# Cross attention of a six-stage decoder block: projections as three rounded products, with the scaling of the probabilities moved from VectorE to ScalarE

## The chip, the core and the metric

One core of a Trainium2 chip runs the whole program in one launch. The metric is the device time of the launch in microseconds, the median of several runs. TensorE multiplies matrices, VectorE and ScalarE work on 128 partitions of rows, POOL (GpSimd) does small vector work and issues stores, SP (SyncE) issues most transfers. Data are float32.

## What is computed

The input x is 4 batches of 512 rows with 512 features; a context has 512 rows of 256 features. Six stages follow each other, each followed by a residual sum and a layer norm: linear attention, a state-space scan, a ternary feed-forward net, attention over the batch axis, cross attention to the context, and a gated feed-forward net whose weights are looked up in a table of 16 values. The change is in the cross attention (16 heads of 128):

```python
q = (hidden_states @ Wq).reshape(B, Sq, H, D)
k = (encoder_hidden_states @ Wk).reshape(B, Skv, H, D)
v = (encoder_hidden_states @ Wv).reshape(B, Skv, H, D)
q = rmsnorm(q, gq)
k = rmsnorm(k, gk)
scores = jnp.einsum('bqhd,bkhd->bhqk', q, k) * scale
attn = jax.nn.softmax(scores, axis=-1)
out = jnp.einsum('bhqk,bkhd->bqhd', attn, v)
out = out.reshape(B, Sq, H * D)
return out @ Wo
```

## The kernel before

The program is written per engine. Each engine runs its instructions in the order written, and they wait for each other by semaphores. The cross attention (in the code the branch `stages >= 4`, semaphore index 3) goes over the 4 batches c and in each over 16 heads hh.

TensorE, for a batch: keys and values of the first group of four heads (`keys(0)`, `values(0)`, four tiles of 128x512 each, two products a tile), four transposed tiles of x, `queries(0)` (four products), `turn_keys(0)`, `query_squares(0)`. Then for each head: `scores(hh)` (four tiles, into banks 4 to 7), `queries(hh + 1)`, `weighted(hh - 1)` (the product of the previous head's probabilities and values), after heads 1, 5 and 9 `values` of the next group, `turn_keys(hh + 1)`, `query_squares(hh + 1)`, `turn_weights(hh)` (16 transposes of the probabilities p4), and after heads 2, 6 and 10 `keys` of the next group. After head 15 the output projection adds, for each head, four products of oT with a tile `woh` of Wo (line 828). Banks 0 to 2 are a ring for everything but the scores; the table TILES4 gives each tile its number in the ring, and `bank4` waits until the tile three before has been copied out (`a_done`).

ScalarE copies the ring's tiles out (`bring`, line 898) in the same order, and computes the four exponentials of a head (line 1098) with the sum of each row. In a head its order is: exponentials, square and copy of the next queries, copy of the previous head's output oT, values if any, next turned keys kr, four tiles pT of turned probabilities, keys if any.

VectorE, in a head: four maxima (line 1509), each with the bias for the exponential (1513), four reciprocals of the sums (1518), each with the scaling of one tile of p4 (1520), after heads 3, 7 and 11 the scaling of the next group's keys (1494, which `turn_keys` waits for), a piece of the last stage's table look-up (`look_up`, lines 1442 to 1456), the mean square of the next queries (1500), and after heads 2, 6 and 10 the key norms (1483, 1485). POOL raises the mean squares to the power -1/2 for queries (1661) and keys (1654).

SP loads the whole of Wq, Wk and Wv before the stage, the context of the batch, the indices of each look-up, and the tiles of Wo, two ahead.

The order of TensorE and of ScalarE in a head, as written (lines 807 on and 1108 on):

```python
# TensorE
scores(hh)
queries(hh + 1)
weighted(hh - 1)
turn_keys(hh + 1); query_squares(hh + 1)
turn_weights(hh)
# ScalarE
exps(hh)
queries(hh + 1)
bring(oT[:, hh - 1, :], got("o", hh - 1))
turned_keys(hh + 1)
for k in range(NT):
    bring(pT[:, k, :], got("pT", hh, k))
```

## Time and profile before

| | |
|---|---|
| three runs | 2971.68, 2980.09, 2981.98 us, median 2980.09 |
| profiled execution | 2983.97 us, span 2982.3 us |
| TensorE, weight loads | 2723.2 us (91%), 1492.2 us (50%) |
| VectorE, ScalarE, POOL | 1976.1 us (66%), 1107.4 us (37%), 637.5 us (21%) |
| DMA | 145.34 MB, 49 GB/s on average |
| chain that ended last | TensorE 62%, VectorE 19%, issue 10%, POOL 5%, ScalarE 2% |

The busy time of an engine is the time in which it had an instruction in work; matmuls overlap, so the pitch of a series is read from the starts of its rows, not from the length of one. A group in the timeline runs into the next by the end of its last instruction: the start of the next row is the true end. In brackets stands the idle time before a row and who ended it. The cross attention takes about 1360 of the 2982 us, from 1229.6 to 2592.

### The profile page before, as it was taken

The page shows a single profiled execution, that of the slowest core. Times are in us where ns is not written, and L with a number is a line of the kernel's source. Part 1 is how long each engine was busy: PE and PEld are TensorE (multiplying, and loading weights), DVE is VectorE, ACT ScalarE, POOL GpSimd, SP SyncE. Part 2 cuts the span into 40 slices and gives each one's busy share as a digit, 9 for nine tenths or more (in the row PEclk, how much of TensorE's full clock was granted, in tenths as well). Part 3 has the DMA queues.
Part 4 walks back from the last instruction along what each step waited for, and adds up shares of the span by engine and source line. Part 5 has one row for each costly group of instructions (what it writes and reads, how often), then busy time and mean ns, then how long its engine had stood idle before and what let it go on. Part 6 is the DMA issues. An engine that isn't in the chain of part 4 may idle for free.

```text
span 2982.3 us, 28735 instructions
## 1 busy us (share of the span) xinstructions
PE 2723.2 (91%) x8882; PEld 1492.2 (50%) x8882; DVE 1976.1 (66%) x3923; ACT 1107.4 (37%) x2015; POOL 637.5 (21%) x569
## 2 busy tenths in 40 slices
...
DMA packets 67406, 145.34 MB, mean 49 GB/s; under 512 B 8115, under 2 KB 24755, under 8 KB 66230
## 3 DMA queue, kind: packets, MB, share of 16 engines
...
q8 instruction: 75, 1.23, 0.2%
q14 instruction: 77, 0.63, 0.1%
...
## 4 chain that ended last, share of the span: by engine, by line
PE 62%; DVE 19%; issue 10%; POOL 5%; ACT 2%; DMA 1%; SPq 1%; DVEq 0%; POOLq 0%; ACTq 0%
PE bank L492 31%; PE bank L828 7%; DVE h L1249 3%; PE bank L783 3%; POOL h L1586 3%; PE bank L842 3%; PE bank L843 3%; PE bank L846 3%; DVE sm L1509 2%; DVE p L1520 1%; DVE val L1448 1%; PE bank L871 1%; PE bank L612 1%; PE bank L768 1%; PE bank L872 1%
## 5 line engine op out<-in xcount | busy, mean ns | idle before, releaser
L1586 POOL TENSOR_TENSOR h<-du,Bb 128x1024 f32<-128x1024 f32 x128 | 306.3, 2396 | 186.9 <-DVE h L1254 173.4
L1249 DVE TENSOR_TENSOR_SCAN h<-bank,h 128x512 f32<-128x512 f32 x256 | 297.8, 1203 | 21.1 <-POOL h L1586 15.1
L953 ACT ACTIVATE bank<-dt,A 128x512 f32<-128x512 f32 x256 | 176.1, 691 | 329.7 <-DVE h L1249 329.6
L1098 ACT ACTIVATE p<-bank,sm,rq 128x512 f32<-128x512 f32 x256 | 199.1, 778 | 209.9 <-DVE sm L1513 209.9
L492 PE MATMUL bank<-pT,v 128*128 128x512 f32 x512 | 237.3, 607 | 2.9 <-ACT pT L898 2.9
L1661 POOL TENSOR_TENSOR rq<-rq,mhalf 128x4 f32<-128x4 f32 x64 | 65.6, 1024 | 791.0 <-DVE rq L1500 791.0
L209 POOL TENSOR_SCALAR rstd<-mv 128x1 f32<-128x1 f32 x96 | 25.3, 264 | 975.4 <-DVE mv L203 975.4
L492 PE MATMUL bank<-xT,wxq 128*128 128x512 f32 x512 | 230.6, 593 | 3.2 <-ACT xT L898 3.2
L828 PE MATMUL bank<-woh,oT 128*128 128x512 f32 x512 | 223.5, 597 | 9.6 <-DMA woh<-in_Wo 7.6
L492 PE MATMUL bank<-kr,q 128*128 128x512 f32 x512 | 230.6, 593 | 0.0
L612 PE MATMUL bank<-h,ident 128*128 128x512 f32 x256 | 151.0, 674 | 83.4 <-DVE h L1254 83.3
L1509 DVE TENSOR_REDUCE sm<-bank 128x1 f32<-128x512 f32 x256 | 175.3, 685 | 33.9 <-PE bank L492 33.7
L1456 DVE COPY_PREDICATED val<-msk,val 128x258 f32<-128x258 int32 x448 | 173.3, 448 | 27.9 <-DVE val L1456 0.2
L1541 DVE TENSOR_TENSOR h<-bank,sg 128x512 f32<-128x512 f32 (+1 forms) x44 | 30.4, 690 | 226.8 <-PE bank L846 226.8
L1254 DVE TENSOR_TENSOR h<-h,Cb 128x1024 f32<-128x1024 f32 x128 | 174.0, 1359 | 6.6
L1448 DVE TENSOR_SCALAR val<-msk,lx,le 128x258 uint32<-128x258 uint32 x512 | 171.6, 410 | 7.9 <-DVE msk L1444 1.4
L828 PEld LDWEIGHTS bank<-woh,oT 128*128 128x128 f32 x512 | 97.2, 191 | 135.2 <-issue 107.5
L492 PEld LDWEIGHTS bank<-pT,v 128*128 128x128 f32 x512 | 99.5, 195 | 129.0 <-issue 124.7
L492 PEld LDWEIGHTS bank<-xT,wxq 128*128 128x128 f32 x512 | 96.9, 190 | 124.7 <-issue 120.5
L195 DVE TENSOR_TENSOR rsum<-bank,xc 128x512 f32<-128x512 f32 x64 | 43.9, 687 | 170.2 <-PE bank L828 165.4
L898 ACT ACTIVATE pT<-bank 128x512 f32<-128x512 f32 x256 | 132.8, 602 | 42.2 <-PE bank L783 42.2
L492 PEld LDWEIGHTS bank<-kr,q 128*128 128x128 f32 x512 | 93.2, 190 | 97.6 <-issue 97.6
...
## 6 DMA issues: line engine op xcount, KB each, us to landing
...
x_dram<-xo POOLq DMA_DIRECT2D x16, 1024.0 KB, 4.7
xc<-x_dram SPq DMA_DIRECT2D x16, 1024.0 KB, 5.2
woh<-in_Wo SPq DMA_DIRECT2D x64, 256.0 KB, 2.7
...
xc<-in_x SPq DMA_DIRECT2D x4, 1024.0 KB, 7.4
```

Of the source, the lines that this page charges most:

```text
L492: m = pe.matmul(dst, l, r, start=(k == 0), stop=(k == len(pairs) - 1))
L612: pe.matmul(bank[4 + et][:, :], ident[:, :], h[:, U % HR, 0, :], start=(w == 0), stop=False)
L828: m = pe.matmul(bank[4 + t][:, :], oT[:, hh, t * P:(t + 1) * P], woh[:, hh % 2, :], start=(hh == 0), stop=(hh == XH - 1))
L898: act.activation(dst, src, ACT.Copy, **more).then_inc(a_done, 1)
L953: act.activation(bank[2 + n][:, :], dt[:, et, :], ACT.Exp, scale=A[:, et, 2 * w + n:2 * w + n + 1]).then_inc(dA_ready, 1)
L1098: act.activation(p4[:, t, :], bank[4 + t][:, :], ACT.Exp, bias=sm4[:, 4 + t:5 + t], scale=rq[:, hh % 2, 1, t:t + 1], accum_out=sm4[:, 8 + ...
L1249: dve.tensor_tensor_scan(h[:, s, n, :], bank[2 + n][:, :], h[:, s, n, :], 0.0, ALU.mult, ALU.add).then_inc(scanned, 1)
L1254: dve.tensor_tensor(h[:, s, :, :], h[:, s, :, :], Cb[:, w % 2, :, :], ALU.mult).then_inc(hC_ready, 1)
L1448: dve.tensor_scalar(val[:, j, :].bitcast(U32), msk[:, 0, :].bitcast(U32), lx[:, j:j + 1], le[:, j:j + 1], ALU.bitwise_and, ALU.bitwise_xor ...
L1456: dve.copy_predicated(val[:, s, :], msk[:, b, :], val[:, s + (1 << (b - 1)), :]).then_inc(lut_step, 1)
L1509: dve.tensor_reduce(sm4[:, t:t + 1], bank[4 + t][:, :], AX.X, ALU.max).then_inc(max_ready, 1)
L1586: pool.tensor_tensor(h[:, U % HR, :, :], du[:, et:et + 1, :].to_broadcast([P, 2, S]), Bb[:, w % 2, :, :], ALU.mult).then_inc(dBu_ready, 1)
```

## The change

1. Every product of the query, key and value projections, and in batches 0 to 2 of the output projection, becomes three matmuls of rounded operands (type fp32r): high times high, high times low, low times high. High is the rounded operand, low what is left of it, rounded too. Scores and weighted values stay float32.
2. The weights are not held whole any more. In batch 0 those of a head (queries) or group (keys, values) are loaded, rounded on ScalarE (`round_wxq`, `round_wxk`, `round_wxv`), the rest is subtracted on VectorE (`wxq_rest` and so on), and both parts are stored in DRAM; batches 1 to 3 fetch them back (`back_wxq`, `back_wxkv`).
3. The context is split a batch ahead (after head 12), x when it has been turned (`x3_rest`; the fourth turned tile waits for the first subtraction), and oT and Wo head by head in front of the output (`round_out`, `out_rest`), two deep.
4. The scaling of the probabilities moves from VectorE to ScalarE (`scales`).
5. POOL's loop over the batches is written out for this stage.

ScalarE's order in an ordinary head before, word for word (p_127 are the probabilities p4, sm the row statistics):

```order
L1098 ACTIVATE p_127,sm_129<-bank,sm_129,rq 128x512 [waits nmax_ready] x4
L1088 ACTIVATE sq<-bank 128x512 [waits a_full]
L898 ACTIVATE q_122<-bank 128x512
L898 ACTIVATE oT<-bank 128x512 [waits a_full]
L898 ACTIVATE kr<-bank,g_136 128x512 [waits a_full,g2_ready]
L898 ACTIVATE pT<-bank 128x512 [waits a_full] x4
```

And of the same engine in a head of the last three batches now:

```order
L1240 ACTIVATE p_131,sm_133<-bank,sm_133,rq 128x512 [waits nmax_ready] x4
L1230 ACTIVATE sq<-bank 128x512 [waits a_full]
L1040 ACTIVATE q_123<-bank 128x512
L1040 ACTIVATE oT<-bank 128x512 [waits a_full]
L1246 ACTIVATE p_131<-p_131,sm_133 128x512 [waits rs_ready] x4
L1040 ACTIVATE kr<-bank,g_140 128x512 [waits a_full,g2_ready]
L1040 ACTIVATE pT<-bank 128x512 [waits a_full] x4
```

The four scalings of the probabilities stand between the copy of oT and the turned keys.

VectorE in head 1 of batch 0 now, from the last bias to the next head's first maximum, without the waits (wxq and wxq_s are the query weights as loaded and in two parts; the table look-up is L1640 to L1654):

```order
L1744 SCALAR_TENSOR_TENSOR sm_133<-sm_133,rq 128x1
L1749 RECIPROCAL sm_133<-sm_133 128x1 x4
L1702 TENSOR_TENSOR wxq_s<-wxq,wxq_s 128x512
L1640 TENSOR_SCALAR msk<-idx 128x258
L1642 TENSOR_SCALAR msk<-idx 128x258 x3
L1646 TENSOR_SCALAR val<-msk,lx,le 128x258 x8
L1654 COPY_PREDICATED val<-msk,val 128x258 x7
L1706 TENSOR_TENSOR wxk_s<-wxk,wxk_s 128x1024
L1698 TENSOR_SCALAR rq<-bank 128x4
L1740 TENSOR_REDUCE sm_133<-bank 128x1
```

The subtraction of the query weights (L1702), which waits for ScalarE's rounding, stands ahead of the look-up, where before the scaling of p4 alternated with the reciprocals.

The same on ScalarE in batch 0: the rounding that VectorE waits for.

```order
L1240 ACTIVATE p_131,sm_133<-bank,sm_133,rq 128x512 [waits nmax_ready] x4
L1230 ACTIVATE sq<-bank 128x512 [waits a_full]
L1040 ACTIVATE q_123<-bank 128x512
L1040 ACTIVATE oT<-bank 128x512 [waits a_full]
L1246 ACTIVATE p_131<-p_131,sm_133 128x512 [waits rs_ready] x4
L1253 ACTIVATE wxq_s<-wxq 128x512 [waits wxq_stored1,wxq_loaded1]
```

It comes after the four scalings, with a wait for its load and for the store of what its buffer held.

The diff, cut to what matters here:

```diff
+def load_wxq(n):
+    hh = n % XH
+    if n >= 2:
+        sp.wait_ge(wxq_split, START + n - 1)
+    sp.dma_start(wxq[:, n % 2, :, :], io["Wq"].rearrange("(k p) n -> p k n", p=P)[:, :, hh * P:(hh + 1) * P])\
+        .then_inc(wxq_loaded[n % 2], 16)
+def store_wxq(n):
+    sp.wait_ge(wxq_split, START + n + 1)
+    sp.dma_start(wq_dram[n, :, :], wxq_s[:, n % 2, :, :, :].rearrange("p e k n -> p (e k n)").bitcast(F32)).then_inc(wxq_stored[n % 2], 16)
+def store_wxkv(n):
+    sp.wait_ge(wxv_split, START + n + 1)
+    sp.dma_start(wkv_dram[n, 0, :, :], wxv_s[:, :, :, :].rearrange("p e k n -> p (e k n)").bitcast(F32)).then_inc(wxv_stored, 16)
+    sp.wait_ge(wxk_split, START + n + 1)
+    sp.dma_start(wkv_dram[n, 1, :, :], wxk_s[:, :, :, :].rearrange("p e k n -> p (e k n)").bitcast(F32)).then_inc(wxk_stored, 16)
+def back_wxq(c, hh):
+    if hh >= 2:
+        sp.wait_ge(a_done, START + A0[3] + after(c, PER_A[3], TILES4["q", hh - 2] + 1))
+    else:
+        sp.wait_ge(a_done, START + A0[3] + after(c - 1, PER_A[3], TILES4["q", XH + hh - 2] + 1))
+    sp.wait_ge(wxq_stored[hh % 2], START + 16 * (XH // 2))
+    sp.dma_start(wxq_s[:, hh % 2, :, :, :].rearrange("p e k n -> p (e k n)").bitcast(F32), wq_dram[hh, :, :]).then_inc(wxq_back[hh % 2], 16)
...
-sp.wait_ge(wo_used, START + after(c, XH - 1, max(0, hh - 1)))
+sp.wait_ge(o_split, START + min(after(c, XH, max(0, hh - 1)), (B - 1) * XH))
+if c == B - 1 and hh >= 2:
+    sp.wait_ge(wo_used, START + after(c, XH - 1, hh - 1))
 sp.dma_start(woh[:, hh % 2, :], io["Wo"][hh * P:(hh + 1) * P, :]).then_inc(wo_loaded[hh % 2], 16)
...
+if c == 0:
+    if hh == 0:
+        store_wxq(0)
+        store_wxkv(0)
+    if hh + 1 < XH:
+        store_wxq(hh + 1)
+    if hh + 2 < XH:
+        load_wxq(hh + 2)
+    if hh % 4 == 3 and hh // 4 + 1 < GROUPS:
+        store_wxkv(hh // 4 + 1)
+    if hh % 4 == 3 and hh // 4 + 2 < GROUPS:
+        load_wxv(hh // 4 + 2)
+        load_wxk(hh // 4 + 2)
+if c + (hh + 2) // XH in range(1, B):
+    back_wxq(c + (hh + 2) // XH, (hh + 2) % XH)
+if hh == 0 and c + 1 < B:
+    load_ctx(c + 1)
+if hh == 0 and c:
+    back_wxkv(c, 1)
+if hh in (3, 7) and c:
+    back_wxkv(c, hh // 4 + 2)
+if hh == 12 and c + 1 < B:
+    back_wxkv(c + 1, 0)
...
+def three4(dst, pairs, inc):
+    for n, (l, r) in enumerate(pairs):
+        m = pe.matmul(dst, l, r, start=(n == 0), stop=(n == len(pairs) - 1))
+    m.then_inc(inc, 1)
...
 def queries(hh):
+    if c:
+        pe.wait_ge(wxq_back[hh % 2], START + 16 * after(c - 1, XH // 2, hh // 2 + 1))
+    else:
+        pe.wait_ge(wxq_split, START + hh + 1)
+    pe.wait_ge(x3_split, START + after(c, KD, KD))
     d = bank4("q", hh)
-    group(d[:, :], [(wxq[:, k, hh * P:(hh + 1) * P], xT[:, k, :]) for k in range(KD)], a_full)
+    three4(d[:, :], [p for k in range(KD) for p in (
+        (wxq_hi[:, hh % 2, k, :], x_hi3[:, k, :]), (wxq_lo[:, hh % 2, k, :], x_hi3[:, k, :]),
+        (wxq_hi[:, hh % 2, k, :], x_lo3[:, k, :]))], a_full)
...
 for k in range(KD):
+    if k == 3:
+        pe.wait_ge(x3_split, START + after(c, KD, 1))
...
+if c < B - 1:
+    pe.wait_ge(o_split, START + after(c, XH, hh + 1))
+    for t in range(NT):
+        tt = slice(t * P, (t + 1) * P)
+        pe.matmul(bank[4 + t][:, :], o_hi3[:, hh % 2, tt], w_hi3[:, hh % 2, :], start=(hh == 0), stop=False)
+        pe.matmul(bank[4 + t][:, :], o_hi3[:, hh % 2, tt], w_lo3[:, hh % 2, :], start=False, stop=False)
+        m = pe.matmul(bank[4 + t][:, :], o_lo3[:, hh % 2, tt], w_hi3[:, hh % 2, :], start=False, stop=(hh == XH - 1))
+        if hh == XH - 1:
+            m.then_inc(v_full, 1)
+    if hh < XH - 1:
+        m.then_inc(wo_used, 1)
+    continue
...
+def scales(hh):
+    for t in range(NT):
+        act.wait_ge(rs_ready, START + after(c, 4 * XH, 4 * hh + t + 1))
+        act.activation(p4[:, t, :], p4[:, t, :], ACT.Copy, scale=sm4[:, 12 + t:13 + t]).then_inc(p_ready, 1)
+def round_wxq(n):
+    act.wait_ge(wxq_loaded[n % 2], START + 16 * (n // 2 + 1))
+    if n >= 2:
+        act.wait_ge(wxq_stored[n % 2], START + 16 * (n // 2))
+    act.activation(wxq_hi[:, n % 2, :, :], wxq[:, n % 2, :, :], ACT.Copy).then_inc(wxq_rounded, 1)
...
+def round_out(hh):
+    act.wait_ge(wo_loaded[hh % 2], START + 16 * after(c, XH // 2, hh // 2 + 1))
+    if hh >= 2:
+        act.wait_ge(wo_used, START + after(c, XH - 1, hh - 1))
+    act.wait_ge(a_done, START + A0[3] + after(c, PER_A[3], TILES4["o", hh] + 1))
+    act.activation(o_hi3[:, hh % 2, :], oT[:, hh, :], ACT.Copy)
+    act.activation(w_hi3[:, hh % 2, :], woh[:, hh % 2, :], ACT.Copy).then_inc(o_rounded, 1)
+if c == 0:
+    round_ctx(0)
+    round_wxk(0)
+    round_wxv(0)
+    round_wxq(0)
+    round_wxq(1)
 keys(0)
 values(0)
...
         bring(oT[:, hh - 1, :], got("o", hh - 1))
+    scales(hh)
+    if c == 0 and hh + 2 < XH:
+        round_wxq(hh + 2)
+    if c == 0 and hh % 4 == 0 and hh // 4 + 1 < GROUPS:
+        round_wxv(hh // 4 + 1)
+    if c == 0 and hh % 4 == 1 and hh // 4 + 1 < GROUPS:
+        round_wxk(hh // 4 + 1)
     if hh % 4 == 1 and hh // 4 < 3:
         values(hh // 4 + 1)
     if hh + 1 < XH:
...
         bring(pT[:, k, :], got("pT", hh, k))
     if hh % 4 == 2 and hh // 4 < 3:
         keys(hh // 4 + 1)
+    if hh == 12 and c + 1 < B:
+        round_ctx(c + 1)
+if c < B - 1:
+    round_out(0)
+    round_out(1)
 bring(oT[:, XH - 1, :], got("o", XH - 1))
+if c < B - 1:
+    for hh in range(2, XH):
+        round_out(hh)
...
+def wxq_rest(n):
+    dve.wait_ge(wxq_rounded, START + n + 1)
+    dve.tensor_tensor(wxq_lo[:, n % 2, :, :], wxq[:, n % 2, :, :], wxq_hi[:, n % 2, :, :], ALU.subtract).then_inc(wxq_split, 1)
...
+def x3_rest():
+    for k in range(KD):
+        dve.wait_ge(a_done, START + A0[3] + after(c, PER_A[3], TILES4["x", k] + 1))
+        dve.tensor_tensor(x_lo3[:, k, :], bank[TILES4["x", k] % 3][:, :], x_hi3[:, k, :], ALU.subtract).then_inc(x3_split, 1)
+def out_rest(hh):
+    dve.wait_ge(o_rounded, START + after(c, XH, hh + 1))
+    dve.tensor_tensor(o_lo3[:, hh % 2, :], oT[:, hh, :], o_hi3[:, hh % 2, :], ALU.subtract)
+    dve.tensor_tensor(w_lo3[:, hh % 2, :], woh[:, hh % 2, :], w_hi3[:, hh % 2, :], ALU.subtract).then_inc(o_split, 1)
+if c == 0:
+    ctx_rest(0)
+    wxk_rest(0)
+    wxv_rest(0)
+    wxq_rest(0)
+    wxq_rest(1)
 key_norms(0)
+x3_rest()
 key_scale(0)
 query_mean(0)
 for hh in range(XH):
...
         n = 4 * hh + t
         dve.wait_ge(p_exp, START + after(c, 4 * XH, n + 1))
         dve.reciprocal(sm4[:, 12 + t:13 + t], sm4[:, 8 + t:9 + t]).then_inc(rs_ready, 1)
-        dve.wait_ge(rs_ready, START + after(c, 4 * XH, n + 1))
-        dve.tensor_scalar(p4[:, t, :], p4[:, t, :], sm4[:, 12 + t:13 + t], None, ALU.mult).then_inc(p_ready, 1)
+    if c == 0 and hh + 2 < XH:
+        wxq_rest(hh + 2)
     if hh % 4 == 3 and hh < XH - 1:
         key_scale(hh // 4 + 1)
     look_up(c, hh)
+    if c == 0 and hh % 4 == 0 and hh // 4 + 1 < GROUPS:
+        wxv_rest(hh // 4 + 1)
+    if c == 0 and hh % 4 == 1 and hh // 4 + 1 < GROUPS:
+        wxk_rest(hh // 4 + 1)
     if hh + 1 < XH:
         query_mean(hh + 1)
     if hh % 4 == 2 and hh // 4 < 3:
         key_norms(hh // 4 + 1)
+    if hh == 12 and c + 1 < B:
+        ctx_rest(c + 1)
+if c < B - 1:
+    for hh in range(XH):
+        out_rest(hh)
```

## Rows read from the trace of the kernel before

**Rows 1.** Busy time by stretch (start:end, length, each engine, clock, DMA): batch 0.
```profile
1229.00:1566.00 337.00, 328.39 (x1105) 170.44 (x1104) 223.20 (x642) 142.38 (x292) 34.15 (x41) 1.00 0.12 36
```

**Rows 2.** Chain of waits (start us, us, what), and TensorE's timeline at two scores.
```profile
1511.49 55.20 PE bank L828 x128
...
1253.90 3.68 PE L492 MATMUL bank<-kr,q 128*128 128x512 f32 x8
...
1494.42 3.60 PE L492 MATMUL bank<-kr,q 128*128 128x512 f32 x8
```

**Rows 3.** TensorE timeline (start us, us, instructions), an ordinary head.
```profile
1654.10 3.60 PE L492 MATMUL bank<-kr,q 128*128 128x512 f32 x8
...
1657.53 3.60 PE L492 MATMUL bank<-xT,wxq 128*128 128x512 f32 x8
...
1665.65 1.98 PE L783 MATMUL bank<-ident,p 128*128 128x128 f32 x16
...
1667.46 3.60 PE L492 MATMUL bank<-kr,q 128*128 128x512 f32 x8
```

**Rows 4.** ScalarE timeline of the same head.
```profile
1659.46 0.78 ACT L1098 ACTIVATE p<-bank,sm,rq 128x512 f32<-128x512 f32 x1 [4.44 <-DVE sm L1513]
...
1662.61 0.59 ACT L1088 ACTIVATE sq<-bank 128x512 f32<-128x512 f32 x1
...
1664.60 0.60 ACT L898 ACTIVATE oT<-bank 128x512 f32<-128x512 f32 x1 [0.92 <-PE bank L492]
...
1665.10 0.69 ACT L898 ACTIVATE kr<-bank,g 128x512 f32<-128x512 f32 x1
```

**Rows 5.** VectorE timeline of the same head.
```profile
1657.63 0.68 DVE L1509 TENSOR_REDUCE sm<-bank 128x1 f32<-128x512 f32 x1
...
1664.10 0.29 DVE L1442 TENSOR_SCALAR msk<-idx 128x258 int32<-128x258 int32 x1
...
1670.82 0.15 DVE L1500 TENSOR_SCALAR rq<-bank 128x4 f32<-128x4 f32 x1
```

**Rows 6.** TensorE timeline, last stage: rounded matmuls.
```profile
2615.28 0.40 PE L871 MATMUL bank<-wdn_hi,h_hi 128*128 128x512 f32 x1
...
2618.04 0.40 PE L842 MATMUL bank<-y_hi,wg_hi 128*128 128x512 f32 x1
```

**Rows 7.** ScalarE timeline: two activations with a scale, and a rounding copy.
```profile
171.44 1.29 ACT L953 ACTIVATE bank<-dt,A 128x512 f32<-128x512 f32 x2
...
2605.44 0.63 ACT L1173 ACTIVATE h_hi<-h 128x512 fp32r<-128x512 f32 x1 [7.76 <-DVE h L1541]
```

**Rows 8.** Instruction groups (count, busy us, mean ns, idle before), and one 128x1024 VectorE row.
```profile
L1483 DVE TENSOR_TENSOR rsum<-kt 128x512 f32<-128x512 f32 x64 | 44.2, 690 | 39.2 <-ACT kt L898 38.7
...
L1485 DVE TENSOR_REDUCE kss<-rsum 128x4 f32<-128x512 f32 x64 | 43.9, 686 | 2.2
...
150.28 1.23 DVE L1254 TENSOR_TENSOR h<-h,Cb 128x1024 f32<-128x1024 f32 x1
```

**Rows 9.** TensorE, VectorE and POOL timelines at the starts of batches 0 and 1.
```profile
1229.63 7.03 PE L492 MATMUL bank<-wxk,ctx 128*128 128x512 f32 x16
...
1235.30 0.69 DVE L1483 TENSOR_TENSOR rsum<-kt 128x512 f32<-128x512 f32 x1
...
1580.12 2.93 POOL L1654 TENSOR_TENSOR kss<-kss,mhalf 128x16 f32<-128x16 f32 x1 [4.28 <-DVE kss L1488]
```

**Rows 10.** DMA issues (count, KB each, median us to landing).
```profile
xc<-x_dram SPq DMA_DIRECT2D x16, 1024.0 KB, 5.2
...
woh<-in_Wo SPq DMA_DIRECT2D x64, 256.0 KB, 2.7
```

**Rows 11.** TensorE after waits, and busy time of two stretches with the granted clock.
```profile
2559.81 32.86 PE L828 MATMUL bank<-woh,oT 128*128 128x512 f32 x72 [3.85 <-DMA woh<-in_Wo]
...
1501.00:1511.00 10.00, 6.16 (x26) 3.15 (x24) 9.26 (x30) 4.48 (x12) 0.00 (x0) 1.00 0.13 44
...
2560.00:2568.00 8.00, 8.00 (x15) 3.34 (x15) 0.00 (x0) 0.00 (x0) 0.00 (x0) 0.79 0.38 121
```

More of the change, by code:

```diff
@@ L748, in values @@
                         def values(g):
+                            pe.wait_ge(ctx_split, START + c + 1)
+                            if c:
+                                pe.wait_ge(wxv_back, START + 16 * after(c - 1, GROUPS, g + 1))
+                            else:
+                                pe.wait_ge(wxv_split, START + g + 1)
                             for t in range(NT):
                                 d = bank4("v", g, t)
-                                group(d[:, :], [(ctx4[:, k, t * P:(t + 1) * P], wxv[:, k, g * 512:(g + 1) * 512]) for k in range(KC)], a_full)
+                                tt = slice(t * P, (t + 1) * P)
+                                three4(d[:, :], [p for k in range(KC) for p in (
+                                    (ctx_hi[:, k, tt], wxv_hi[:, k, :]), (ctx_hi[:, k, tt], wxv_lo[:, k, :]), (ctx_lo[:, k, tt], wxv_hi[:, k, :]))], a_full)
@@ L1103, in _ @@
                         for k in range(KD):
[L1104 removed]
+                            bring(x_hi3[:, k, :], got("x", k))
                         queries(0)
@@ L1640, in attention, with cross, key_rms @@
                 store_chunk(2, c)
+            def cross(c):
+                def key_rms(g):
+                    pool.wait_ge(k_mean, START + after(c, 4, g + 1))
+                    kf = kss[:, :, :].rearrange("p t n -> p (t n)")
+                    pool.tensor_tensor(kf, kf, mhalf[:, :], ALU.pow).then_inc(k_pow, 1)
+                key_rms(0)
+                for hh in range(XH):
+                    r = rq[:, hh % 2]
+                    pool.wait_ge(rq_raw, START + after(c, XH, hh + 1))
+                    pool.tensor_tensor(r[:, 0, :], r[:, 0, :], mhalf[:, 0:4], ALU.pow).then_inc(rq_one, 1)
+                    pool.wait_ge(rq_one, START + after(c, XH, hh + 1))
+                    hold(pool)
+                    pool.tensor_scalar(r[:, 1, :], r[:, 0, :], float(XD) ** -0.5, None, ALU.mult).then_inc(rq_pow, 1)
+                    if hh % 4 == 3 and hh < XH - 1:
+                        key_rms(hh // 4 + 1)
+                for t in range(NT):
+                    ln_pool(pool, T0[3] + after(c, PER_T[3], t), t % 2)
+                store_chunk(3, c)
             for n in range(1, min(stages, 5)):
@@ L1646, in _ @@
                     continue
+                if n == 3:
+                    for c in range(B):
+                        cross(c)
+                    continue
                 with pool.Fori(0, B // 2) as i:
```

111 lines of the change are left out of this document (83 added, 28 removed).

## The prediction

> **What bounds the kernel now.** I read the busy times by stretch first. In batch 0 of the cross attention TensorE is busy for 328 of 337 us at full clock, VectorE for 223 and ScalarE for 142 [rows 1]. The chain of waits then shows that each of the four output projections is one unbroken piece of TensorE, 55.20 us in batch 0 [rows 2]. The TensorE timeline of an ordinary head shows no gap either: from one head's scores (1654.10) to the next (1667.46) 13.36 us [rows 3]. Last I read ScalarE and VectorE in the same head [rows 4, 5]: VectorE is nearly as full as TensorE (first maximum 1657.63, look-up done 1670.82). So less matmul time can only help while what each head waits for on ScalarE and VectorE still arrives under it. That is where this change is decided.
>
> **Price of a product.** A float32 product of 128x512 takes 3.43/4 = 0.858 us (four scores from 1654.10 to 1657.53 [rows 3]). A rounded matmul takes (2618.04 - 2615.28)/12 = 0.230 us [rows 6]; three take 0.69, with 0.696 used below. Each replaced product saves 0.162: queries 2.79 instead of 3.43 a head, a group of keys or of values 5.57 instead of 6.87. The Trainium skill (FP8 and Floating Point Precision, TensorE Precision Notes) says that true float32 is four passes, so three would cost 0.75 x 0.858 = 0.644; by that alone the sum below would be some 16 us lower. The measured row has more overhead per pass, and it decides.
>
> **Ordinary head, batches 1 to 3.** What moves to ScalarE is the scaling of the probabilities, four instructions, and the order shows where: behind the copy of the previous head's output. That copy waits for the weighted product: scores 3.43, queries 2.79, weighted 3.43 = 9.65 after the scores began. Add 0.20 for the signal and 0.50 for the copy (the next one starts 0.50 later [rows 4]): 10.35. A scaling on ScalarE is not in the trace. Bounds: 0.53 each (rounding copy, 0.63 long [rows 7], the next starting 0.10 before its end) and 0.68 (the exponential with scale and bias, 0.78 less 0.10 [rows 4]). I take 0.60, since two activations with a scale per partition take 1.29 back to back [rows 7]; four are 3 x 0.60 + 0.72 = 2.52, ending at 12.87. TensorE, done with its squares at 10.9, waits 2 us, then transposes for 1.82 [rows 3]: 14.74, against 13.36. **The saved 0.65 becomes a loss of 1.4.** VectorE is rid of the scalings and not the bound here.
> Head 0 has no weighted product; the scalings follow the query copies (7.4): 11.8. A head with values hides them: 3.43 + 2.79 + 3.43 + 5.57 + 3.07 = 18.3 against 20.2 (13.36 and eight products, 6.87). A head with keys is 14.74 + 5.57 = 20.3, as before. Scores of head 0 to scores of head 15: 11.8 + 3 x 18.3 + 3 x 20.3 + 8 x 14.74 = 245.5, against 240.5 (1253.90 to 1494.42 [rows 2]): **+5.0 a batch, +15.0**.
>
> **Batch 0: a ring.** Here VectorE subtracts head hh+2's rounded query weights after head hh's reciprocals and ahead of its look-up. The rounding itself is behind the four scalings on ScalarE. So look-up, maxima of the next head, exponentials, output copy, scalings, rounding and subtraction follow each other, with TensorE beside them. From the first maximum: exponentials begin after 1.83 and take 3.15, two query copies 0.98 (1657.63, 1659.46, 1662.61 [rows 4, 5]), output copy 0.50, scalings 2.40, rounding 0.63, subtraction 0.70 with its signal (a float32 tensor operation of this size is 0.69 [rows 8]), look-up 6.72 (1664.10 to 1670.82), 0.1 to the next maximum: 17.0 us a head. Per four heads the ring also takes key scaling 4 x 0.60 + 0.1, two subtractions of 128x1024 at 1.15 (1.23 long [rows 8]) and key norms 4 x 1.32 + 0.1 = 5.4: 78.2. In a key-scaling head the next keys cannot be turned before the end of this, so TensorE stands some 7 us. Twelve rings (head 0's without output copy) take 234.1, two more 34.0, the subtraction of the next context 1.15; 1.1 ahead of the first maximum and 10.8 from head 14's to the scores of head 15 make 281: **+40.5**.
>
> **Starts.** Batch 0's keys waited for nothing (1229.63). Now VectorE, free at 1235.30, first subtracts context and key weights, 2.3: keys at 1237.6, plus 11.14 for keys and values, transposes with the new wait on VectorE for the fourth, until 1253.0, queries 2.79, key turn and copies to scores: 1258.0 against 1253.90 [rows 2, 9]: **+4.1**. In the others x's four subtractions (2.4) end before POOL's power of 2.93, which begins 13.4 us after the output [rows 2, 9], releases the key scaling; shorter queries and tail give -0.4 each, **-1.2**.
>
> **Ends.** The output of a head is 12 x 0.232 = 2.78 on TensorE. Its two-deep pipeline needs two roundings 1.16, two subtractions 1.30 and the signals, 0.4, in the time of the other slot: 2.78 to 2.9. The weight load comes 2.7 after its issue [rows 10], just in time. 16 heads: 46.0 against 55.04, and 0.2 later at its start through the last scalings: -8.8 for each of batches 0 to 2, **-26.4**. Batch 3 keeps float32: **+0.2**.
>
> Costed at nothing: stores and fetches of split weights (0.5 to 1 MB, a head ahead; 1 MB lands in 5.2 us [rows 10] and a head is 13 or more; without that cover each would cost up to 5 us), POOL's loop written out, ScalarE's first roundings (five, some 4 us, while VectorE is still in the stage before; uncovered they would delay the first keys by that).
>
> **Sum:** 4.1 - 1.2 + 15.0 + 40.5 - 26.4 + 0.2 = +32.2. The profiled execution took 2983.97 (span 2982.3), so it would be 3016.2; the median of the runs is 3.9 lower, so I forecast 3012. A measurement of this kernel tells about 0.5% (15 us) from no change.
>
> **Rivals.**
> A. *TensorE stays the bound everywhere.* Then each batch saves 128 x 0.162 = 20.7, four 83, the outputs 26: about 2873. It holds if the last scaling ends before the squares do (10.9) and the ring of batch 0 is under TensorE's 12.7 a head. ScalarE's rows leave 0.55 us for four scalings and the ring's rows add to 17.0. Chance 0.05.
> B. *Batch 0 escapes the ring*: roundings run ahead, and only ScalarE's extra copies delay it (0.2 to 1.1 a head, +13 over the batch instead of 40.5): 2985, no change. The program order speaks against it. Chance 0.09.
> C. *TensorE's clock falls.* In the last output projection, after waits of up to 3.85 us, 72 matmuls took 32.86 us instead of 30.9 with a granted clock of 0.79 (part of it at 1.2, the rest at 2.4 GHz), while a stretch of 10 us with 3.8 idle kept 1.00 [rows 11]. In batches 1 to 3 the gaps are 2 us. In batch 0 they are 3 to 7; if each of 15 heads lost 1.8 us on the path, the time is 3039. The Trainium skill (TensorE: Matmul & The Clock Gate, What's actually happening) has 1.2 GHz as the default that only activity lifts, and the trace agrees so far. Since TensorE has slack in the ring, most of it should be covered. Chance 0.14.
> D. *Weight transfers come late in batch 0*, where a 1 MB pair of stores and loads joins the query weights: the load of head hh+2 is issued one look-up late and the rounding waits, 3 us for each of six heads: 3030. Chance 0.07.
>
> **Numbers.** The forecast has 0.65. The bounds of a scaling move the sum by -16 (0.53) or +13 (0.68): four times 0.07 or 0.08 in some 50 heads. The output pipeline at 2.78 or 3.1 moves it by -4 or +10. The two unknowns together reach 2992 downward; upward C and D set 3044. Slower by over 0.5% (above 2995): the forecast, C and D, 0.86, less 0.02 for its lower edge: 0.84; within: B and that edge, 0.11; faster: A, 0.05.
>
> **What would show it.** TensorE in batches 1 to 3 idle about 2 us ahead of the transposes of the probabilities, released by ScalarE's scaling; heads 14.7 apart. In batch 0 VectorE waiting on ScalarE's rounding ahead of the look-up, group of four heads 78 us, TensorE idle on scaled keys. Outputs of 46 us. Wrong, if scores stay 13.4 apart or less, if VectorE does not wait in batch 0, or if the projection stays near 55.

## The result and the profile after

| | before | after |
|---|---|---|
| median (range) | 2981.03 us (2971.68 to 2983.29, four runs) | 3086.45 us (3084.16 to 3087.91, four runs) |
| ratio | | 1.0359, 95% interval 1.034 to 1.0379 |
| span of the profiled execution | 2982.3 us | 3081.7 us |
| TensorE, VectorE, ScalarE busy | 2723.2, 1976.1, 1107.4 us | 2696.0, 1950.4, 1345.8 us |

The kernel became slower by 3.6%: +105 us at the median, +99.4 in the span of the profiled executions. I forecast slower, by 32 us, and gave a range that ended at 3044: the sign was right, but I forecast only a third of the loss.

The same stretches in both profiled executions, from the starts of the rows of TensorE's timeline (us; "heads" is from the scores of head 0 to those of head 15):

| | predicted change | batch 0 | batch 1 | batch 2 | batch 3 |
|---|---|---|---|---|---|
| output of the batch before to scores of head 0 | +4.1, then -0.4 each | +7.3 (whole start) | 22.33 to 23.20 | 22.33 to 23.07 | 22.33 to 24.09 |
| heads | +40.5, then +5.0 each | 240.5 to 296.9 | 240.5 to 260.0 | 240.8 to 257.6 | 240.5 to 256.0 |
| head 15 to the output projection | +0.2 | 17.1 to 18.8 | 19.9 to 18.8 | 20.2 to 21.1 | 21.7 to 22.9 |
| output projection | -9.0 (last +0) | 55.0 to 46.1 | 55.0 to 46.8 | 55.0 to 46.9 | 66.3 to 69.8 |

The heads cost 56.4 + 19.5 + 16.8 + 15.5 = 108 us instead of the 55.5 predicted. That is 53 of the 67 us by which the spans missed the sum of the prediction; most of the rest is in the starts and in the last projection. The first part of the page of the kernel after. ScalarE has 238 us more to do, VectorE 26 less, TensorE, in a longer span, 27 less:

```profile
PE 2696.0 (87%) x9586; PEld 1688.4 (55%) x9586; DVE 1950.4 (63%) x3807; ACT 1345.8 (44%) x2395; POOL 640.7 (21%) x569
```

Busy time by stretch, the columns of [rows 1]: the first row answers to [rows 1]; then the heads of batch 0, its output projection, and the heads of batches 1 to 3.

```profile
1229.00:1566.00 337.00, 279.77 (x1085) 191.17 (x1083) 211.99 (x593) 191.27 (x370) 36.42 (x41) 0.89 0.31 102
...
1261.00:1559.00 298.00, 250.81 (x982) 171.72 (x982) 187.80 (x541) 178.09 (x344) 30.88 (x34) 0.89 0.26 86
1576.00:1623.00 47.00, 46.01 (x193) 35.15 (x193) 19.75 (x33) 16.73 (x29) 0.00 (x0) 1.00 0.33 103
1646.00:1906.00 260.00, 236.91 (x978) 162.48 (x979) 173.31 (x521) 166.01 (x322) 28.77 (x35) 0.94 0.25 81
1995.00:2253.00 258.00, 234.91 (x978) 161.91 (x978) 173.06 (x521) 166.87 (x324) 28.81 (x35) 0.95 0.26 82
2344.00:2600.00 256.00, 232.91 (x981) 159.63 (x981) 172.00 (x520) 165.14 (x323) 28.77 (x35) 0.96 0.22 70
```

TensorE is idle for 23 us in the heads of each later batch and for 47 us in batch 0, and the granted clock is below 1.00. Before, all four were full (239 of 240 us) at 1.00.

The end of two heads that follow each other on TensorE (heads 6 and 7 of batch 2, the keys between them left out); it answers to the transposes of [rows 3].

```profile
2107.45 0.60 PE L890 MATMUL bank<-ident,kt 128*128 128x128 f32 x4
2107.89 0.95 PE L897 MATMUL bank<-ones,sq 128*128 128x1 f32 x8
2110.75 3.52 PE L912 MATMUL bank<-ident,p 128*128 128x128 f32 x16 [1.91 <-ACT p L1246]
...
2129.37 0.60 PE L890 MATMUL bank<-ident,kt 128*128 128x128 f32 x4
2129.80 0.95 PE L897 MATMUL bank<-ones,sq 128*128 128x1 f32 x8
2132.66 2.00 PE L912 MATMUL bank<-ident,p 128*128 128x128 f32 x16 [1.91 <-ACT p L1246]
```

Both heads show the wait that was predicted: 1.91 us, ended by ScalarE's last scaling (L1246). But behind the same wait the 16 transposes took 3.52 us once and 2.00 the other time (3.17 and 1.84 to the start of the next row). The granted clock says why (same columns as above):

```profile
2105.50:2109.00 3.50, 3.34 (x17) 2.01 (x16) 3.21 (x10) 1.34 (x3) 0.00 (x0) 1.00 0.00 0
2109.00:2114.00 5.00, 3.25 (x17) 3.25 (x17) 1.06 (x4) 4.01 (x7) 1.26 (x2) 0.70 0.43 104
...
2131.00:2137.00 6.00, 4.34 (x22) 2.93 (x23) 4.85 (x14) 4.25 (x8) 1.04 (x2) 1.00 0.06 8
```

In the first the clock fell from 2.4 to 1.2 GHz for part of the stretch. An ordinary head that keeps its clock takes 14.79 us (predicted 14.74), the others 15.2 to 16.2. The falls are not spread at random: all nine heads with keys (2, 6 and 10 of the three batches) took 21.7 to 21.9 us instead of the predicted 20.3, and heads 3 and 7 kept 14.8 in all six cases.

ScalarE in an undisturbed head answers to [rows 4]:

```profile
2215.63 0.60 ACT L1040 ACTIVATE oT<-bank 128x512 f32<-128x512 f32 x1 [2.35 <-PE bank L594]
2216.12 2.54 ACT L1246 ACTIVATE p<-p,sm 128x512 f32<-128x512 f32 x4
2218.57 0.67 ACT L1040 ACTIVATE kr<-bank,g 128x512 f32<-128x512 f32 x1
```

ScalarE idles 2.35 us before the copy of oT, and the scalings, whose last reciprocal VectorE had done at 2212.13, are queued behind it. Four took 2.54 (predicted 2.52).

Batch 0 on VectorE, three of the waits ahead of the query subtraction (L1702), and what TensorE does when the last of them ends:

```profile
1355.75 0.69 DVE L1702 TENSOR_TENSOR wxq_s<-wxq,wxq_s 128x512 fp32r<-128x512 f32 x1 [7.83 <-ACT wxq_s L1253]
...
1393.30 0.69 DVE L1702 TENSOR_TENSOR wxq_s<-wxq,wxq_s 128x512 fp32r<-128x512 f32 x1 [5.62 <-ACT wxq_s L1253]
...
1415.37 0.69 DVE L1702 TENSOR_TENSOR wxq_s<-wxq,wxq_s 128x512 fp32r<-128x512 f32 x1 [4.75 <-ACT wxq_s L1253]
```

```profile
1418.52 1.12 PE L890 MATMUL bank<-ident,kt 128*128 128x128 f32 x4 [6.78 <-DVE kt L1692]
1419.43 1.71 PE L897 MATMUL bank<-ones,sq 128*128 128x1 f32 x8
1420.99 3.65 PE L912 MATMUL bank<-ident,p 128*128 128x128 f32 x16
```

The ring is there: VectorE waits for ScalarE's rounding, and TensorE waits 6.78 us for the scaled keys. Then turned keys, squares and transposes run at 1.2 GHz.

### The profile page after: what moved, and what is told of

The parts are those of the page before. It is cut to its first block and busy times, and to the rows that moved or that the text cites. A ratio compares the mean times of both kernels' runs of the same rounds, so it can differ in the third digit from the quotient of the medians.

```text
span 3081.7 us, 30680 instructions
## 1 busy us (share of the span) xinstructions
PE 2696.0 (87%) x9586; PEld 1688.4 (55%) x9586; DVE 1950.4 (63%) x3807; ACT 1345.8 (44%) x2395; POOL 640.7 (21%) x569
## 5 line engine op out<-in xcount | busy, mean ns | idle before, releaser
L912 PE MATMUL bank<-ident,p 128*128 128x128 f32 x1024 | 174.5, 341 | 98.1 <-ACT p L1246 96.1
L594 PE MATMUL bank<-kr,q 128*128 128x512 f32 x512 | 244.4, 622 | 0.0
L714 PE MATMUL bank<-h,ident 128*128 128x512 f32 x256 | 152.9, 681 | 81.9 <-DVE h L1452 81.8
L912 PEld LDWEIGHTS bank<-ident,p 128*128 128x128 f32 x1024 | 153.5, 178 | 107.9 <-ACT p L1246 103.2
L844 PE MATMUL bank<-x_hi,wxq_s 128*128 128x512 f32 x512 | 189.6, 452 | 6.4 <-DVE x_lo L1719 6.4
L1654 DVE COPY_PREDICATED val<-msk,val 128x258 f32<-128x258 int32 x448 | 173.7, 450 | 28.9 <-DVE val L1654 1.1
L1040 ACT ACTIVATE pT<-bank 128x512 f32<-128x512 f32 x256 | 143.0, 599 | 48.0 <-PE bank L912 46.8
L1246 ACT ACTIVATE p<-p,sm 128x512 f32<-128x512 f32 x256 | 163.1, 713 | 0.0
L594 PEld LDWEIGHTS bank<-kr,q 128*128 128x128 f32 x512 | 100.9, 207 | 100.9 <-issue 99.9
L715 PE MATMUL bank<-h,ident 128*128 128x512 f32 x256 | 141.0, 634 | 0.0
## 6 DMA issues: line engine op xcount, KB each, us to landing
woh<-in_Wo SPq DMA_DIRECT2D x64, 256.0 KB, 2.7
```

Source lines behind the costliest of these rows:

```text
L594: m = pe.matmul(dst, l, r, start=(k == 0), stop=(k == len(pairs) - 1))
L844: m = pe.matmul(dst, l, r, start=(n == 0), stop=(n == len(pairs) - 1))
L912: m = pe.transpose(d[:, t * P:(t + 1) * P], p4[:, t, k * P:(k + 1) * P], ident[:, :])
L1040: act.activation(dst, src, ACT.Copy, **more).then_inc(a_done, 1)
L1246: act.activation(p4[:, t, :], p4[:, t, :], ACT.Copy, scale=sm4[:, 12 + t:13 + t]).then_inc(p_ready, 1)
L1654: dve.copy_predicated(val[:, s, :], msk[:, b, :], val[:, s + (1 << (b - 1)), :]).then_inc(lut_step, 1)
```

## The experiments

Two theories stood at the start. Mine: the loss is one of *place* (the scalings stand behind a copy that waits for TensorE; the subtraction stands ahead of the look-up), plus a clock that falls in the waits so made. The rivals: ScalarE has too much to do wherever the scalings stand; batch 0 is long because of late transfers; the transposes are slow for another reason than the clock. The columns "batch 0" to "3" are the times from the scores of head 0 to those of head 15, from the timelines:

| kernel | median us | ratio to before (95%) | batch 0 | 1 | 2 | 3 |
|---|---|---|---|---|---|---|
| before | | 1 | 240.5 | 240.5 | 240.8 | 240.5 |
| after | 3086.45 | 1.0359 (1.034 to 1.0379) | 296.9 | 260.0 | 257.6 | 256.0 |
| scalings early | 2975.86 | 0.9977 (0.9967 to 0.9987) | 282.9 | 233.5 | 232.2 | 231.6 |
| subtraction late | 3051.12 | 1.0228 (1.0198 to 1.0258) | 269.8 | 256.2 | 259.7 | 251.5 |
| both moves | 2930.35 | 0.9818 (0.9799 to 0.9836) | 237.2 | 232.3 | 234.0 | 233.2 |
| gap filled | 3052.84 | 1.0234 (1.0217 to 1.0251) | 300.7 | 249.4 | 249.4 | 247.7 |
| scaling on VectorE | 2955.64 | 0.9908 (0.9888 to 0.9928) | 257.5 | 226.3 | 226.3 | 225.5 |
| same, subtraction late | 2926.75 | 0.9814 (0.9789 to 0.9838) | 234.7 | 226.3 | 226.4 | 225.6 |
| before, scaling on ScalarE | 3150.36 | 1.0563 (1.0539 to 1.0588) | 282.7 | 281.1 | 282.6 | 282.6 |
| both moves, queries first in 3, 7, 11 | 2927.35 | 0.9801 (0.9775 to 0.9827) | 234.1 | 232.3 | 234.0 | 231.6 |
| both moves, queries first in 4, 8, 12 | 2909.36 | 0.9756 (0.9737 to 0.9776) | 233.9 | 227.1 | 228.6 | 227.9 |
| scalings shared | 2919.25 | 0.9785 (0.9768 to 0.9801) | 237.1 | 230.9 | 231.4 | 230.8 |
| shared, queries first in 13 | 2914.55 | 0.9766 (0.9749 to 0.9784) | 236.8 | 229.0 | 227.8 | 228.2 |

The kernel before ran at 2980.0 to 2982.6 beside each group.

### 1. Scalings right behind the exponentials

```diff
 exps(hh)
+scales(hh)
 if hh + 1 < XH:
     queries(hh + 1)
 if hh:
     bring(oT[:, hh - 1, :], got("o", hh - 1))
-scales(hh)
```

> ScalarE's four scalings of the probabilities moved from behind the copy of the previous head's output to right behind the exponentials, ahead of the next query copies; all else as changed. My theory (the PLACE of the scalings makes TensorE wait 1.9 us, and the wait makes its clock fall): exponentials end 6.4 us after the scores began, scalings 8.9, query copies 9.9, so the squares (10.1) and transposes (10.9) find everything done. In batches 1 to 3 no gap, clock 1.00, ordinary heads 12.8, value and key heads 18.3 to 18.5, scores of head 0 to scores of head 15 about 225 instead of 260, 258 and 256: -97. Batch 0 keeps its 297, since the same pieces follow each other there. Total about 2989 (2980 to 3000). Rival 1 (ScalarE simply has too much to do with the scalings, wherever they stand): batches 1 to 3 unchanged, 3086. Rival 2 (the gap goes, but the rounded products themselves run below full clock): heads of 14 or more, about 3040.

-111 us by a change of place alone, with as many instructions on each engine: rival 1 and rival 2 are out. Ordinary heads took 12.80 and value heads 18.17 as expected. I missed two things. Batches 1 to 3 took 232 to 234, not 225: heads 4, 8 and 12 took 14.4 to 16.0 (see 6). And batch 0 lost 14 of its 297, where I expected none. The traces of the two kernels show where they went. The ring had held ScalarE's wait for the weighted product too, up to 2.35 us ahead of the copy of oT and 12.8 us over batch 0, and the scalings now fill that time. VectorE's 14 waits for the rounding add up to 77.0 us in the changed kernel and 64.0 in this one. Head 8 of batch 0 on ScalarE in the changed kernel, and the subtraction of head 4 in this one, which answers to the row with 7.83 above:

```profile
1434.52 0.60 ACT L1040 ACTIVATE oT<-bank 128x512 f32<-128x512 f32 x1 [2.35 <-PE bank L594]
```

```profile
1350.91 0.69 DVE L1702 TENSOR_TENSOR wxq_s<-wxq,wxq_s 128x512 fp32r<-128x512 f32 x1 [5.38 <-ACT wxq_s L1253]
```

### 2. The subtraction behind the look-up in batch 0

```diff
-if c == 0 and hh + 2 < XH:
-    wxq_rest(hh + 2)
 if hh % 4 == 3 and hh < XH - 1:
     key_scale(hh // 4 + 1)
 look_up(c, hh)
+if c == 0 and hh + 2 < XH:
+    wxq_rest(hh + 2)
```

> Batch 0 alone: VectorE's subtraction of the query weights moved from ahead of the table look-up to behind it (the key scaling stays ahead of both); ScalarE and TensorE as changed. My theory (a RING over ScalarE's rounding, the subtraction, the look-up and the next maxima sets batch 0): the 5 to 8 us that VectorE waits ahead of the subtraction lie behind the look-up and mostly vanish; batch 0 becomes like batches 1 to 3 plus ScalarE's rounding: ordinary heads 15.2 to 16.5, scores of head 0 to scores of head 15 about 268 (255 to 275) instead of 297. Batches 1 to 3 unchanged. Total about 3057 (3044 to 3062). Rival (batch 0 is long because the loads and stores of the split weights are late, or because of the clock): 297 stays within 5 us, total 3086.

-35 us, 27 of them in batch 0 (269.8 against 268 expected), most of the rest in batches 1 to 3, whose heads came out between 251.5 and 259.7 with nothing changed in them: waits of 1.91 us are followed by slow transposes in some heads and not in others, and not in the same ones as in the execution above. The waits ahead of the subtraction shrank to about 1.1 us:

```profile
1385.62 0.69 DVE L1702 TENSOR_TENSOR wxq_s<-wxq,wxq_s 128x512 fp32r<-128x512 f32 x1 [1.08 <-ACT wxq_s L1253]
```

So most of batch 0's excess over the others was the ring and not the transfers, whose number and size are as before the move.

### 3. Both moves

The diffs of 1 and 2 together.

> Both moves together: scalings right behind the exponentials on ScalarE, and the query subtraction behind the look-up on VectorE in batch 0. My theory: batches 1 to 3 as with the first move alone (about 225 from the scores of head 0 to those of head 15), batch 0 now bound by TensorE with a little from ScalarE's roundings, 230 to 245 instead of 297. Total about 2928 (2910 to 2945), faster than the kernel before by 1.7%. Rival (the two causes are one, or each move's gain is taken by the other engine): no less than the sum of the first two alone, 2955 or more.

As expected, 2930.35, faster than the kernel before by 1.8%. The two moves alone gave 111 and 35 us, together 156.

### 4. The gap filled with idle products

```diff
+if c and (hh % 4 in (0, 2) or hh == 13):
+    pe.wait_ge(p_exp, START + after(c, 4 * XH, 4 * hh + 4))
+    for n in range(2):
+        pe.matmul(bank[4][:, :], q4[:, hh % 2, 0:P], kr[:, hh % 2, :], start=True, stop=True)
 turn_weights(hh)
```

> The changed kernel with two idle float32 products of 128x512 (1.7 us, into score bank 4, whose content has been read by then and is overwritten by the next scores) on TensorE ahead of the transposes of the probabilities, in batches 1 to 3, in the heads where TensorE waited there (heads 0, 4, 8, 12, 2, 6, 10, 14, 13); nothing else. The work added lies in the wait. My theory (part of the loss is the CLOCK, which falls in the wait, so that the 16 transposes took 2.6 to 3.5 instead of 1.8 us and the scores 4.2 to 4.5 instead of 3.4): clock 1.00 throughout batches 1 to 3, all ordinary heads 14.8, key heads 20.4, scores of head 0 to scores of head 15 about 246 to 249 instead of 260, 258 and 256: -30, total about 3056 (3048 to 3065). Rival (transposes and scores are slow there for another reason, such as ScalarE's copies or the weight loads): unchanged or a little longer, 3086 to 3095.

Work was added and the kernel became faster, by 34 us. The products lie in the time in which TensorE would have waited, and nobody reads what they write. The end of a filled head, and the clock over the heads of batch 2 (0.99 in all three batches, 0.94 to 0.96 without the filling):

```profile
2219.36 1.96 PE L948 MATMUL bank<-kr,q 128*128 128x512 f32 x4
2221.40 2.00 PE L912 MATMUL bank<-ident,p 128*128 128x128 f32 x16
```

```profile
1989.00:2239.00 250.00, 242.88 (x1015) 158.56 (x1014) 173.15 (x520) 165.47 (x324) 28.81 (x35) 0.99 0.27 84
```

The filled ordinary heads take 14.80, but for two that followed a slow one (16.0), and the heads with keys 20.4 instead of 21.9. Heads 3 and 7, which were left unfilled and had kept their clock in the changed kernel, now took 15.2 to 16.3 in five of six cases. Between the two profiled executions, 25.5 us apart, the heads of batches 1 to 3 gained 27.1 us and those of batch 0 lost 3.8. So the transposes were slow by the clock, and the rival is out.

### 5. Which part of the change costs

The scaling back on VectorE, all else as changed:

```diff
 dve.reciprocal(sm4[:, 12 + t:13 + t], sm4[:, 8 + t:9 + t]).then_inc(rs_ready, 1)
+dve.wait_ge(rs_ready, START + after(c, 4 * XH, n + 1))
+dve.tensor_scalar(p4[:, t, :], p4[:, t, :], sm4[:, 12 + t:13 + t], None, ALU.mult).then_inc(p_ready, 1)
```

and `scales(hh)` taken out of ScalarE.

> The changed kernel with the scaling of the probabilities back on VectorE, alternating with the reciprocals as in the kernel before; rounded products, splits and the subtraction ahead of the look-up stay. My theory (the moved scaling costs batches 1 to 3 their gain and lengthens the ring of batch 0 by its own 2.4 us a head): batches 1 to 3 have no gap ahead of the transposes and clock 1.00, scores of head 0 to scores of head 15 228 to 240 each; batch 0 keeps a ring shorter by 2.4 a head, about 261 (255 to 270). Total about 2976 (2960 to 2992). Rival (the rounded products with their splits are what costs, and the scaling is a detail): above 3040.

Better than I expected: 2955.64. Rounded products, splits, stores and fetches together *gain* 0.9% over the kernel before; the moved scaling alone costs the changed kernel 131 us. The heads of batch 1 are full again, at full clock:

```profile
1610.00:1837.00 227.00, 223.00 (x982) 149.90 (x982) 195.07 (x571) 127.06 (x264) 28.43 (x33) 1.00 0.30 91
```

The converse, the kernel before with nothing but the scaling moved to where the change has it:

```diff
 bring(oT[:, hh - 1, :], got("o", hh - 1))
+for t in range(NT):
+    act.wait_ge(rs_ready, START + after(c, 4 * XH, 4 * hh + t + 1))
+    act.activation(p4[:, t, :], p4[:, t, :], ACT.Copy, scale=sm4[:, 12 + t:13 + t]).then_inc(p_ready, 1)
...
-dve.wait_ge(rs_ready, START + after(c, 4 * XH, n + 1))
-dve.tensor_scalar(p4[:, t, :], p4[:, t, :], sm4[:, 12 + t:13 + t], None, ALU.mult).then_inc(p_ready, 1)
```

> The kernel BEFORE with one part of the change alone: the scaling of the probabilities on ScalarE behind the copy of the previous head's output. Products stay float32, weights whole. My theory: oT is copied at 10.3 + 0.7 = 11.0 after the scores began, scalings to 13.5, transposes to 15.45: ordinary heads 15.45 instead of 13.36 at full clock, more where the clock falls in the 2 us gap, key heads 22.3, value heads stay 20.2, head 0 about 12. Scores of head 0 to scores of head 15: 265 at full clock, 278 with the loss of clock seen in the changed kernel, against 240.5, in all four batches. Total about 3130 (3095 to 3150), longer than with the whole change (3086). Rival (ScalarE has room enough at 37% of the span): within 1% of the kernel before.

At 3150.36 it lies just beyond the expected range and is the slowest of all, with float32 products and no splits. Its ordinary heads take 17.05 to 17.08 us (heads 3, 7 and 11: 16.5 to 17.05): 15.45 at full clock as worked out, and 1.6 more behind the wait, 1.3 of it in the transposes and 0.4 in the scores. The granted clock over the heads of batch 1 is 0.93. Behind the wait stand slow transposes and slow scores:

```profile
1890.03 0.95 PE L768 MATMUL bank<-ones,sq 128*128 128x1 f32 x8
1892.88 3.30 PE L783 MATMUL bank<-ident,p 128*128 128x128 f32 x16 [1.90 <-ACT p L1115]
1895.97 3.98 PE L492 MATMUL bank<-kr,q 128*128 128x512 f32 x8
```

And the scaling on VectorE together with the diff of experiment 2:

> As the run before, and in batch 0 the query subtraction behind the look-up. My theory: the ring is gone, but VectorE, with scalings, look-up, subtractions and key work, is now the bound of batch 0: 4 x 14.0 for four heads, and 2.5 + 5.4 + 2.3 for key scaling, key norms and the wide subtractions, 66 us per four heads, so 245 to 252 from the scores of head 0 to those of head 15. Batches 1 to 3 as in the run before. Total about 2963 (2945 to 2980), slower than the version with both moves (2930). Rival (with either engine the scaling costs nothing once the order is right): 2930 or less.

My figure for batch 0 was wrong (234.7, not 245 to 252) and the rival's time holds: 2926.75, no different from both moves with the scalings on ScalarE. VectorE had more room than I gave it. Its scaling is a short one, as the groups of the kernel before show (mean 486 ns); ScalarE's is 713 ns long in the mean of the changed kernel, and 2.54/4 = 0.635 us each where four overlap:

```profile
L1520 DVE TENSOR_SCALAR p<-p,sm 128x512 f32<-128x512 f32 x256 | 124.5, 486 | 9.1
```

### 6. The gap that was left, and one head too early

The version with both moves, TensorE in head 4 of batch 1, and ScalarE there:

```profile
1655.50 1.05 PE L897 MATMUL bank<-ones,sq 128*128 128x1 f32 x8 [1.38 <-ACT q L1040]
```

```profile
1651.94 2.55 ACT L1246 ACTIVATE p<-p,sm 128x512 f32<-128x512 f32 x4
1654.38 0.58 ACT L1230 ACTIVATE sq<-bank 128x512 f32<-128x512 f32 x1
1654.86 0.58 ACT L1040 ACTIVATE q<-bank 128x512 f32<-128x512 f32 x1
```

VectorE comes late out of key norms and key scaling, the exponentials end 8.1 us after the scores began, and with the scalings first the query copies, which the squares need, end last. I let ScalarE copy the queries ahead of the scalings, in heads 3, 7 and 11:

```diff
 exps(hh)
+if hh in (3, 7, 11):
+    queries(hh + 1)
 scales(hh)
-if hh + 1 < XH:
+if hh not in (3, 7, 11, 15):
     queries(hh + 1)
```

> Both moves, and in heads 3, 7, 11 (and only there) ScalarE copies the next queries ahead of the scalings, since in the version with both moves TensorE waited 1.38 us there for that copy ahead of its squares, because VectorE comes late out of key norms and key scaling. My theory: the squares start when the keys are turned, the transposes wait only for the scalings, 0.8 us earlier; with a little less loss of clock 1 to 2 us for each of 12 heads. Total about 2918 (2905 to 2930). Rival (the scalings end at the same time either way and the clock falls as before): 2930, no difference from the version with both moves.

No difference from both moves (the intervals overlap): I had miscounted, the gap is in the head *behind* the one that scales the keys. The head times show it: in batch 1 head 3 went from 12.79 to 12.73, head 4 from 14.37 to 14.44. In the right heads, the same diff with (4, 8, 12):

> Both moves, and in heads 4, 8 and 12 (only there) ScalarE copies the next queries ahead of the scalings. The run before this changed the order in heads 3, 7 and 11, one head too early: the gap of 1.38 us ahead of the squares is in the head after the key scaling, where VectorE's maxima come 2 us late. My theory: there the copies end at 9.2 after the scores began, so squares follow the turned keys at once; scalings end at 11.6 and the transposes start 0.9 earlier, with two short waits instead of one of 1.4. Heads 4, 8 and 12 take 13.5 to 14.2 instead of 14.4 to 16.5, about 1.5 less each: -18, total about 2912 (2900 to 2922). Rival (scalings end the same way and the clock falls in the wait ahead of the transposes instead): 2925 to 2930.

2909.36 at the median, the fastest of all, 2.4% below the kernel before, and by its interval below both moves. In batches 1 to 3 heads 4, 8 and 12 take 13.7 to 13.8 us, and the clock is 1.00 in batch 1 and 0.99 in the others:

```profile
1581.00:1808.00 227.00, 222.55 (x977) 149.66 (x977) 172.72 (x521) 161.72 (x323) 27.69 (x33) 1.00 0.29 91
```

In batch 0 they stay at 14.8 to 15.8; ScalarE's rounding stands there as well, which I did not try to move.

The last two share the scalings by head, VectorE's as in experiment 5 under `if hh < 13`, and on ScalarE:

```diff
 exps(hh)
+if hh >= 13:
+    scales(hh)
 if hh + 1 < XH:
     queries(hh + 1)
```

> Subtraction behind the look-up, and the scalings shared by head: heads 0 to 12 on VectorE with the reciprocals, heads 13 to 15 on ScalarE right behind the exponentials. With all scalings on VectorE heads 13 and 14 took 13.8 and 13.3 instead of 12.7, and from the scores of head 15 to the output it was 19.5 instead of 15.1 (VectorE full, first maximum 4.4 after the scores against 1.1), while with all on ScalarE heads 4, 8, 12 lose 2 to 3. My theory: VectorE catches up over the last three heads, so each batch has the better of both: scores of head 0 to 15 about 225, then 15 to 16.5 to the output. Total about 2905 (2895 to 2915). Rival (VectorE does not catch up in three heads, or ScalarE becomes late there): 2920 to 2930, no difference from either version alone.

At 2919.25 it misses the expected range and comes out a little below the rival's 2920: from the scores of head 15 to the output it is 15.13 in batches 0 to 2 as hoped, but head 13, where the engine changes, takes 17.7 to 18.8 us. VectorE is still late there, and ScalarE's query copy stands behind the scalings, so the same gap came back larger:

```profile
1797.95 1.87 PE L897 MATMUL bank<-ones,sq 128*128 128x1 f32 x8 [3.35 <-ACT q L1040]
1799.68 3.65 PE L912 MATMUL bank<-ident,p 128*128 128x128 f32 x16
```

In the last one `scales(13)` stands behind `queries(14)`:

> As the run before (scalings of heads 0 to 12 on VectorE, 13 to 15 on ScalarE), and in head 13, where the scalings change engine, ScalarE copies the next queries ahead of them. There TensorE waited 3.35 us for that copy ahead of its squares, and squares and transposes then ran at half clock (head 13: 18.8 instead of 12.7), since VectorE, full until then, gives the first maximum late. My theory: with the copies first the squares follow the turned keys, the scalings end 1.0 later than now, at 1797.9 by the trace of that run, and the transposes begin there instead of at 1799.7: head 13 takes 14.7 at full clock, 16.3 with a fall, so 2.5 to 4 less in each of four batches: total about 2906 (2899 to 2912). Rival (the late maxima of head 13 set its end whatever the order): 2916 to 2920.

Head 13 gained 0.5 to 3.1 us a batch and the median 4.7. At 2914.55 the time lies just above the expected range and below the rival's, and its interval overlaps that of the run before. It brings nothing over the version with the queries first in 4, 8 and 12.

## Why the prediction was wrong

**What bounds the kernel**: right. "Less matmul time can only help while what each head waits for on ScalarE and VectorE still arrives under it" is what all runs showed.

**Ordinary head, batches 1 to 3**: the mechanism is right to 0.05 us (scalings behind the copy of oT, 2.54 long, a wait of 1.91 us, 14.79 where the clock holds). The term, +5.0 a batch, was mis-sized: it measured +19.5, +16.8 and +15.5, in the heads with keys (21.9 instead of 20.3) as in the ordinary ones. What failed is one sentence under rival C: a stretch with 3.8 us idle "kept 1.00", so that waits of 2 us seemed harmless, and I put the fall of the clock in batch 0 only. Filling the waits gave back 27 of the 37 us by which these heads exceeded the predicted 245.5.

The evidence was in the trace of the kernel before. [Rows 11] show the end of batch 0. The same place, waits of 2.8 to 3.2 us ahead of the transposes and then the weighted product of head 15, occurs four times, and I read one. The other three, from TensorE's timeline of the kernel before:

```profile
1839.23 2.45 PE L783 MATMUL bank<-ident,p 128*128 128x128 f32 x16 [2.83 <-DVE p L1520]
1842.37 6.21 PE L492 MATMUL bank<-pT,v 128*128 128x512 f32 x8 [0.69 <-ACT pT L898]
...
2177.70 2.91 PE L783 MATMUL bank<-ident,p 128*128 128x128 f32 x16 [3.21 <-DVE p L1520]
2181.30 5.71 PE L492 MATMUL bank<-pT,v 128*128 128x512 f32 x8 [0.69 <-ACT pT L898]
...
2515.45 2.75 PE L783 MATMUL bank<-ident,p 128*128 128x128 f32 x16 [2.84 <-DVE p L1520]
2518.89 5.87 PE L492 MATMUL bank<-pT,v 128*128 128x512 f32 x8 [0.69 <-ACT pT L898]
```

In batch 0 these took 2.00 and 3.70. The granted clock over the same 10 us, 1.00 in [rows 11], is 0.66 in each of the three others:

```profile
1839.00:1849.00 10.00, 8.66 (x24) 4.37 (x24) 6.37 (x20) 2.56 (x5) 0.00 (x0) 0.66 0.04 14
```

The clock had fallen in three of four cases, and the one that I quoted was the fourth.

**Batch 0, the ring**: right in kind (VectorE's waits of 4 to 8 us, TensorE idle 6.78 us on scaled keys, and the moves of experiments 1 to 3 took it apart), short in size: +56.4 instead of +40.5. A group of four heads took 82.8 instead of 78.2. In the key-scaling head turned keys, squares and transposes ran at half clock: 0.91 + 1.56 + 3.45 by the starts of the rows instead of 0.44 + 0.82 + 1.82, 2.8 more on the path. The ring also left out ScalarE's wait for the weighted product: 2.35, 0, 1.25 and 0.38 us in heads 4 to 7, 4.0 of the 4.6 us that their group took too long, and experiment 1, which fills it, gave back 14.0 of the 15.9 us missing in the batch. The two overlap: the scores that the slow rows delay make the wait of 2.35 in the head behind them, so they can't be added. "TensorE has slack in the ring, most of it should be covered" was wrong wherever ScalarE waits for the weighted product, and most of all behind the key-scaling head.

**Starts**: keys began at 1237.98 (1237.6 predicted), but after 6.30 us of idleness at half clock, so that keys and values took 13.82 us instead of 11.14, and batch 0 was +7.3 instead of +4.1:

```profile
1238.00:1243.00 5.00, 5.00 (x12) 3.98 (x13) 3.42 (x5) 0.60 (x1) 0.00 (x0) 0.50 0.57 189
```

The other starts were +0.9, +0.7 and +1.8 instead of -0.4; what made that I did not trace.

**Ends**: 46.1, 46.8 and 46.9 against 46.0: right. Batch 3 was +4.8 instead of +0.2, 3.5 of it in the projection, whose waits for its weights are 8.3 us together (7.6 before) and whose granted clock is 0.93 (0.97 before). Why stays open.

**Rivals**: A and B did not occur as the change stands. A version close to A, TensorE bound in the heads, is what experiment 5 made of it. C occurred, in all batches, and joined my forecast instead of replacing it; that the two add was in no case of mine. D did not: in batch 0 the rounding follows the last scaling at once (scalings from 1390.20, rounding at 1392.65, no wait on a load).

**What would show it**: waits of 1.9 us released by the scaling, VectorE waiting for the rounding and outputs of 46 were all found; 14.7 apart only where the clock held.
